# Flamingo block with sixteen experts: routing spread over the attention loop, expert stage fed by pairs of sequences

## What is computed

```
x = x + tanh(g_xattn) * attention(layernorm(x), ctx, ctx)
    # 16 heads of 16 channels, rope on q and k, keys within 64 tokens, softmax
x = x + tanh(g_ffn) * experts(layernorm(x))
    # per sequence: g = x @ w_router (256 x 16), probs = softmax(g), the top 2 of 16 experts per token
    # pos = how many earlier picks of this sequence went to the same expert
    #       (all first picks, in token order, come before all second picks)
    # a pick with pos < 16 puts the token into slot (expert, pos)
    # h = silu(slots @ w_gate[e]) * (slots @ w_fc[e]);  o = h @ w_proj[e]
    # token = sum of its two picks, each weighted by its probability
```

## Time and profile before

| | |
|---|---|
| Median of 3 runs | 1762.0 us (1760.66 to 1764.96) |
| Profiled execution, its own time | 1754.3 us |
| Span in the profile | 1752.5 us |
| TensorE busy | 1481.3 us (85%) |
| VectorE busy | 1408.6 us (80%) |
| ScalarE busy | 1146.4 us (65%) |
| GpSimd busy | 1086.1 us (62%) |
| Granted TensorE clock, mean | 0.960 |
| Memory traffic | 125.54 MB read, 83.89 MB written |

### The profile page before, as it was taken

One profiled execution on the slowest core, in us unless ns is written; L12 is line 12 of the kernel. 1 busy time (PEld: TensorE's weight loads), 2 busy tenths in 40 slices (PEclk: granted clock), 3 DMA queues, 4 the chain that ended last, 5 costly groups with the idle time before them and its releaser, 6 DMA issues. The chain is left out here.

```text
span 1752.5 us, 50746 instructions
## 1 busy us (share of the span) xinstructions
PE 1481.3 (85%) x16844; PEld 1195.2 (68%) x16844; DVE 1408.6 (80%) x2993; ACT 1146.4 (65%) x2321; POOL 1086.1 (62%) x1490
## 2 busy tenths in 40 slices
PE   3899999999999999999999999982199888888881
PEld 3676667777776676777676677761088888888881
DVE  3788888888888888878888888867878999999984
ACT  3777777777777777777777777764065555555550
POOL 3555656565655656565565656534638887888876
PEclk9999999999999999999999999995589999999995
DMA  3122121212222121212212121430037888888887
GB/s 94 50 76 75 61 89 60 90 60 84 65 67 82 60 90 60 90 60 78 71 62 88 60 90 60 137 119 30 15 106 245 260 261 258 261 273 263 264 261 223
DMA packets 156096, 210.21 MB, mean 120 GB/s; under 512 B 18688, under 2 KB 104832, under 8 KB 156032
## 3 DMA queue, kind: packets, MB, share of 16 engines
q1 hardware_dynamic: 125312, 142.36, 25.9%
q0 software_dynamic: 12288, 33.57, 6.7%
q10 hardware_dynamic: 18432, 33.56, 5.3%
HBM read 125.54 MB, written 83.89 MB: 119 GB/s over the span
## 5 line engine op out<-in xcount | busy, mean ns | idle before, releaser
L506 DVE TRANSPOSE_TENSOR_REDUCE part_max<-ST 128x16 f32<-128x512 f32 x512 | 321.3, 685 | 136.6 <-PE ST L685 136.6
L360 ACT ACTIVATE probs_t<-ST 128x512 f32<-128x512 f32 x512 | 264.4, 604 | 27.6 <-PE ST L700 27.4
L712 PE MATMUL PO<-probs_t,v_aug 128*32 128x128 f32 x4096 | 193.6, 284 | 67.9 <-ACT probs_t L360 55.4
L299 POOL TENSOR_TENSOR k_rot<-k_cos,k_sin 128x256 f32<-128x256 f32 x64 | 47.1, 736 | 268.5 <-DVE k_sin L544 268.5
L712 PEld LDWEIGHTS PO<-probs_t,v_aug 128*32 128x32 f32 x4096 | 88.9, 109 | 161.1 <-ACT probs_t L360 154.0
L1191 ACT ACTIVATE x_hi<-scaled 128x256 fp32r<-128x256 f32 x128 | 53.5, 418 | 214.8 <-DMA scaled<-xn_d 168.5
L401 ACT ACTIVATE at_hi<-F 128x512 fp32r<-128x512 f32 x64 | 38.2, 597 | 187.8 <-PE F L730 187.8
L1260 PE MATMUL GU<-we_hi,s_hi 128*128 128x256 f32 x512 | 155.4, 304 | 0.2 <-DVE s_lo L1250 0.2
L1154 POOL DMA_INDIRECT second<-eo_d,collect_row x128 | 123.0, 961 | 42.2 <-issue 28.6
L1163 POOL TENSOR_TENSOR x_lo<-scaled,x_hi 128x256 fp32r<-128x256 f32 x128 | 118.4, 925 | 49.3 <-ACT x_hi L1191 47.3
L1154 POOL DMA_INDIRECT first<-eo_d,collect_row x128 | 124.4, 972 | 37.3 <-issue 20.6
(11 more groups left out here) (158 smaller groups left out, 5610.7 us busy)
## 6 DMA issues: line engine op xcount, KB each, us to landing
eo_d<-eo ACTq DMA_DIRECT2D x128, 256.0 KB
x_in_sb<-x SPq DMA_DIRECT2D x64, 256.0 KB, 2.8
c_in_sb<-ctx_t SPq DMA_DIRECT2D x64, 256.0 KB, 2.9
xr_sb<-x SPq DMA_DIRECT2D x64, 256.0 KB, 4.0
x_d<-x SPq DMA_DIRECT2D x64, 256.0 KB, 4.0
xn_d<-xn SPq DMA_DIRECT2D x64, 256.0 KB, 4.2
scaled<-xn_d SPq DMA_DIRECT2D x128, 128.0 KB, 4.0
scaled<-x_d SPq DMA_DIRECT2D x128, 128.0 KB
```

Source lines behind the costliest of these rows:

```text
L360: act.activation(probs_t[:, b, i].rearrange("p j q -> p (j q)"), ST[i][:], ACT.Exp) \
L506: dve.tensor_reduce(part_max[:, i, 0], ST[i][:].rearrange("p (c l) -> p c l", l=32), AX_X, ALU.max, apply_transpose=True).then_inc(M["part ...
L712: last = pe.matmul(PO[32 * j:32 * j + 32, i * SEQ:(i + 1) * SEQ], v_aug[:, n.par, b, head], probs_t[:, b, i, j], start=True, stop=True)
```

## The change

Routing goes into attention's steps. Four sequences (two pairs, a `quad`) are routed together, in small instructions of 64 or 128 elements per partition. VectorE does some before `partial_max(s, 1)` (`route_early`) and some at the end of the step, before `partial_max(s + 1, 0)` (`route_late`); GpSimd, ScalarE and TensorE do the others, each one or more steps after what it needs:

```diff
+        def route_early(s):
+            if quad(s, 4):
+                find_first(quad(s, 4))
+                compare(quad(s, 4), 0)
+            if quad(s, 5):
+                expert_of(quad(s, 5), 0)
+            if quad(s, 6):
+                find_second(quad(s, 6))
+                compare(quad(s, 6), 1)
+            if quad(s, 7):
+                expert_of(quad(s, 7), 1)
+            if quad(s, 9):
+                rank_of(quad(s, 9))
+        def route_late(s):
+            if quad(s, 2):
+                find_peak(quad(s, 2))
+            if quad(s, 5):
+                drop_first(quad(s, 5))
+            if quad(s, 7):
+                mark_both(quad(s, 7))
+            if quad(s, 8):
+                ranks_of(quad(s, 8))
```

`quad(s, lag)` is the pair s - lag if that is odd and real, so even lags fall in odd steps. `find_first` is two reductions (sum and maximum), `drop_first` two instructions, the others one each. The one on TensorE comes last in its step, before the next scores:

```diff
+        def rank(s, n):
+            pe.wait_ge(M["marks_done"], n.half + 1)
+            wait_for(pe, M["ranked_done"], n.half)
...
+            pe.matmul(F2[:, 0:width], before[:], one, start=True, stop=True)
+            pe.matmul(F2[:, width:2 * width], ones_b[:], one, start=True, stop=False)
+            pe.matmul(F2[:, width:2 * width], before[:], two, start=False, stop=True).then_inc(M["ranks_done"], 1)
```

`width` is 64. TensorE's `untranspose(n, 1)` waits for `ranked_done` in addition, as both use bank F2. GpSimd's `route` (`less_peak`, twice `code_of`, `place_of`, lags 3, 5, 7, 9) stands between `residual` and `rotate`; ScalarE's `exp_logits` (lag 4) between `normed2` and `attention_head`. In the loop:

```diff
-        for c in range(-4, 2):
+        for c in range(-4, 12):
             step(Pair(0, c))
-        with eng.Fori(1, PAIRS // 2 - 2) as i:
+        with eng.Fori(6, PAIRS // 2 - 2) as i:
...
-        for c in range(PAIRS - 4, PAIRS + 2):
+        for c in range(PAIRS - 4, PAIRS + 9):
```

`routing_block` and `early_softmax` are gone. The expert weights are loaded in steps 4 to 8 (was 60 to 64) and split in steps 63 (`s.beyond == -1`) and 64 (`s.beyond == 0`), on ScalarE (`weight_heads`) and VectorE (`weight_rests`). To have room, attention's buffers that no step after 62 needs share their memory with `we_hi`, and `we_lo` lies over `w_in`. ScalarE's step:

```diff
+            if s.beyond == -1:
+                weight_heads(0, 3)
             if (s - 1).real:
                 attention_head(s - 1)
...
+            if s.beyond == 0:
+                weight_heads(8, 10)
             if (s - 2).real:
                 copy_normed2_t(s - 2)
...
+            if s.beyond == -1:
+                weight_heads(3, 8)
+            if s.beyond == 0:
+                weight_heads(10, CH)
```

VectorE's step:

```diff
                 shift_of(s, 0)
+            if s.beyond == -1:
+                weight_rests(0, 3)
...
+            if s.beyond == 0:
+                weight_rests(7, 8)
+            route_early(s)
...
                 residual_stats(s - 1)
+            if s.beyond == -1:
+                weight_rests(3, 7)
+            if s.beyond == 0:
+                weight_rests(8, CH)
```

```diff
-    LOAD, PICK, DISPATCH, GATE, HIDDEN, OUTPUT, FETCH, COLLECT = -13, -11, -9, 0, 2, 3, 12, 14
+    LOAD, PICK, HEAD, REST, DISPATCH, GATE, HIDDEN, OUTPUT, FETCH, COLLECT = -14, -11, -11, -10, -9, 0, 2, 3, 13, 15
...
+            if on(FETCH) and n.n % 2 == 0:
+                if n.n >= 6:
+                    for k in range(2):
+                        sp.wait_ge(y_out[(n.n + k) % 6], n.n // 6 * 16)
+                sp.dma_start(two(xr, n, 6), D["x1_d"][:, bass.ds(n.n, 2)]).then_inc(x1_in[n.n // 2 % 3], 16)
...
+                act.activation(gate[:, n.slot(2)], GU[n.slot(2)][:].rearrange("p (e f n) -> p e f n", e=2, f=2)[:, :, 0],
+                               ACT.Silu).then_inc(M["gate_done"], 1)
...
-                dve.scalar_tensor_tensor(out=th[:, n.slot(2)], in0=th[:, n.slot(2)], scalar=1.0, in1=gu[:, :, 0],
-                                         op0=ALU.add, op1=ALU.mult).then_inc(M["gated_done"], 1)
...
+                dve.tensor_tensor(flat(two(x_lo, n, 4)), flat(two(x_in_sb, n, 4)), flat(two(x_hi, n, 4)).bitcast(F32),
+                                  ALU.subtract).then_inc(M["x_lo_done"], 1)
```

More of the change, by code:

```diff
@@ L447, in normed2, with exp_logits, weight_heads @@
             last.then_inc(M["xn2_done"], 1)
+        def exp_logits(n):
+            act.wait_ge(M["less_done"], n.half + 1)
+            act.activation(four(scaled, n), four(scaled, n), ACT.Exp).then_inc(M["exp_done"], 1)
+        def weight_heads(first, end):
+            if first == 0:
+                act.wait_ge(M["w_landed"], 16 * (2 * KC + 1))
+                act.wait_ge(M["v_done"], PAIRS)
+                act.wait_ge(M["k_lo_done"], PAIRS)
+                act.wait_ge(M["ct_lo_done"], PAIRS)
+            for c in range(first, end):
+                act.activation(heads[:, c], raw[:, c], ACT.Copy).then_inc(M["heads_done"], 1)
         def step(s):
@@ L732, in transposes @@
             return last
+        weights = [(w_hi[:, w], w_lo[:, w]) for w in range(3)] + [(wo_hi[:], wo_lo[:])]
         def project(F, w, hi, lo, m):
@@ L1073, in expert_block @@
     second = sb("second", [P, 3, DIM])
-    ident, iota = T["ident2"], T["iota"]
-    place, collect_row, weight = T["place"], T["collect_row"], T["weight"]
+    ident, iota = T["ident"], sb("iota_sb", [P, SLOTS])
+    place, collect_row, weight = T["place"], T["code"][:].bitcast(I32), T["prob"]
+    kept, share = T["rank"], T["total"]
     half = EXPERTS * 2 * HID
@@ L1170, in step @@
         def step(unit, on):
-            n = unit(OUTPUT)
-            if on(OUTPUT):
-                act.wait_ge(M["eo_done"], n.n + 1)
-                wait_for(act, eo_out[n.turn(3)], (n - 3).landed(3))
-                act.activation(flat(eo[:, n.turn(3)]), EO[n.slot(2)][:], ACT.Copy).then_inc(M["eo_copied"], 1)
             n = unit(HIDDEN)
@@ L1183, in step @@
             if on(OUTPUT):
+                act.wait_ge(M["eo_done"], n.n + 1)
+                wait_for(act, eo_out[n.turn(3)], (n - 3).landed(3))
+                act.activation(flat(eo[:, n.turn(3)]), EO[n.slot(2)][:], ACT.Copy).then_inc(M["eo_copied"], 1)
+            n = unit(OUTPUT)
+            if on(OUTPUT):
                 act.wait_ge(M["eo_copied"], n.n + 1)
@@ L1186, in step @@
                     .then_inc(eo_out[n.turn(3)], 16)
-            n = unit(PICK)
-            if on(PICK):
-                act.wait_ge(x_in[n.turn(3)], n.landed(3))
-                wait_for(act, M["ds_done"], n.n - 1)
-                act.activation(x_hi[:, n.slot(2)], x_in_sb[:, n.turn(3)], ACT.Copy).then_inc(M["x_hi_done"], 1)
+            n = unit(HEAD)
+            if on(HEAD) and n.n % 2 == 0:
+                act.wait_ge(x_in[n.n // 2 % 2], pair_landed(n, 2))
+                wait_for(act, M["ds_done"], n.n - 2)
+                act.activation(flat(two(x_hi, n, 4)), flat(two(x_in_sb, n, 4)), ACT.Copy).then_inc(M["x_hi_done"], 1)
             n = unit(GATE)
```

520 lines of the change are left out of this document (259 added, 261 removed).

## The result

The changed kernel takes 1751.3 us (median of 4 runs, 1749.8 to 1752.8), the kernel before beside it 1763.0 (1760.7 to 1765.0). The ratio is 0.9936, with a 95% interval of 0.9917 to 0.9954: 0.6% less time, clear of the noise but small, where 1696 was forecast. The profiled execution has a span of 1750.4 us against 1752.5 before. The two spans differ by 2.1 us and the medians by 11.6, since the profiled execution of the kernel before (1754.3 us) was faster than any other run of it here (1756.2 to 1767.3).

What follows compares the result with a forecast made beforehand. Each stage has another limit; full expert units have four resources near 3.5 us. Terms +20 +3 -46.9 +1 +1 -47 +2.5 = -66.4 from 1754.3 give 1688, or 1696 on the median's footing; range 1664 to 1734.

Steps and rivals of the forecast that it cites:

- the routing stage: Between last logits and first pick: 56.4 us replaced by 9.5 (28 small instructions, handoffs, a block end), -46.9 us.
- splitting: Splitting the expert weights moves from the routing stage into steps 63 and 64: +3 us, bounds 0 and 7.
- start, expert start and tail: Setup +1 us, expert start +1, tail +2.5 from collecting one unit later and gathers pacing the end.
- So TensorE is next, with DMA just under it ... I take 3.05: Full expert units: TensorE sets the pace at 2.90 us; with some waits 3.05 instead of 3.53, -47 us.
- The 0.17 us that larger pieces should take off the queues: Expert-unit loads: 2 KB instead of 1 KB pieces cut DMA time per unit from 3.00 to 2.83 us.
- Rival 1: Expert units: DMA keeps the pace, a unit stays at about 3.4 us, total 1730; chance 0.15.
- Rival 4: Expert units: VectorE and GpSimd block each other, 4.2 us a unit, +66 instead of -47, total 1809; chance 0.04.
- Even late: 0.99 less 0.34 less the 0.3 absorbed, 0.35 late: Attention loop, end of even steps: three VectorE instructions overrun their slot by 0.35 us per two steps.
- TensorE's 0.3: Attention loop: three uncovered bf16 routing matmuls with their waits cost TensorE 0.3 us per two steps.
- My 0.33 us per instruction: Attention loop: assumed time of each of 13 small VectorE routing instructions per two steps, between 0.25 and 0.44.
- the five of the odd step: Attention loop, odd early slot: five VectorE instructions take 1.65 us against 1.60, 0.05 late.

Runs made afterwards that it cites:

- e4: Changed kernel with each load of xn2 and x1 issued as two transfers of one sequence instead of one of two: 1748.2 us.
- e8: Changed kernel with gathers issued for the first three sequences only (output not the reference's): 1655.1 us.
- e11: Changed kernel with the second gather left out after the first three sequences (output not the reference's): 1664.3 us.
- e14: Changed kernel with the second gather bringing half a row per token after the first three sequences (output not the reference's): 1673.8 us.
- e16: Changed kernel's attention and routing with the expert units of the kernel before, OUTPUT one unit later (4) and the factor 0.5 restored: 1749.8 us.
- e3: Changed kernel with x1 loaded only for the first six sequences (output not the reference's): 1746.5 us.
- e13: Changed kernel with OUTPUT one unit later (4; FETCH 14, COLLECT 16): 1685.4 us.
- e12: Changed kernel with x_lo on GpSimd again in place of VectorE: 1770.1 us.
- e9: Changed kernel with GpSimd's residual (xb) in even steps waiting for VectorE's marks of the step before: 1737.2 us.
- e15: Changed kernel with GpSimd's residual waiting for marks, rest made after marks, and OUTPUT one unit later: 1663.0 us against 1757.7 for the kernel before, ratio 0.9455.
- e7: Changed kernel with TensorE's three small routing matmuls issued twice: 1752.3 us.
- e6: Changed kernel with drop_first, mark_both and all of route_early placed right after shift_of(s, 0), where GpSimd waits for k_sin: 1866.7 us.
- e2: Changed kernel's attention and routing with the expert units of the kernel before, output weights lacking the factor 0.5: 1750.1 us.
- e5: Kernel before with only the changed kernel's expert stage, turns and buffer layout: 1767.6 us beside 1765.4.
- e1: Changed kernel with drop_first and mark_both moved from the end of even steps to before the second maxima of even steps: 1752.3 us.

## Why the prediction was wrong

The parts at the ends came out: the routing stage -45.3 (forecast -46.9; the small instructions took 7.6 us where I had 9, and 3.5 us of waiting for `iota`, which I did not have, made up for it by luck), splitting +5.2 (3, bounds 0 to 7), start, expert start and tail within 3.1 us each. The stage has one ACT_TABLE_LOAD for Silu, 1.28 us at 1266.52, and none per unit, as the Trainium skill (ScalarE: Activation LUTs, Table sets) had led to expect.

**Expert units: the step that failed is "So TensorE is next, with DMA just under it ... I take 3.05".** Most parts of that step held. The collects take 0.48 us (0.477 to 0.479), VectorE and GpSimd have the slack I gave them, `x_hi` no longer waits for its load, and given one more unit of lag the pace is 2.90, at my lower bound, with DMA at 0.95 (I had said 2.83 of 2.90 us would be busy). The 0.17 us that larger pieces should take off the queues did not come (0.05, and e4 has the same with small ones), but decided nothing. What the sum left out is not a resource but a distance: HT of a unit and its EO lie one turn apart. In the timeline from 1504 on HT's row ends at 1504.83 and EO starts at 1506.55, 1.72 us; `h_hi` starts at 1504.87 and `h_lo` ends at 1506.21:

```profile
1504.45 0.38 PE L1348 MATMUL HT<-ident_sb,gate 128*128 128x128 f32 x2
...
1505.79 0.42 DVE L1277 TENSOR_TENSOR h_lo<-HT,h_hi 128x256 fp32r<-128x256 f32 x1
...
1506.55 0.28 PE L1327 MATMUL EO<-we_hi,h_hi 128*128 128x256 f32 x1
```

Any lateness of over 0.34 us is TensorE's. The distance alone does not hold the pace, since e8, e11 and e14 reach 2.87 with it; it takes the distance and the late signals, at which the prediction had nothing. A list of busy times can't show that; TensorE's waits by line could have, since in the kernel before too they stood ahead of EO, and I had put the whole of the 3.53 down to loads and busy engines. The run with the later OUTPUT and the old units (e16) shows that the old form had a limit of its own at 3.50, with ScalarE waiting for loads. The change took that limit away and met the next one, by coincidence, at the same pace.

Rival 1 gave a unit of 3.4 and a total of 1730, the right sign of the error for a wrong reason: e3 and e13 rule out the traffic as the limit. Rival 4 did not come about: the collects were not stretched with x_lo on VectorE, and e12 shows that they are when it is GpSimd's. (It had gathers running 75% of the time; two of 0.95 us in 3.53 are 54%.)

**Attention: "Even late: 0.99 less 0.34 less the 0.3 absorbed, 0.35 late", and TensorE's 0.3.** Four sizes were off. The three instructions take 1.30 us, not 0.99, since `marks` runs beside `xb`. Nothing is absorbed: 1.30 - 0.34 is 0.96, and the five of the odd step take 609.78 to 611.46, 1.68 against a slot of 1.60, 0.08; together 1.04 of the 1.09 measured. By the same sum e9 gives 0.82 - 0.34 + 0.08 = 0.56 (measured 0.61) and e15 0.59 - 0.34 + 0.08 = 0.33 (0.37). TensorE's matmuls cost nothing (e7). And 24 pairs of steps paid, those of the loop, not 30: 24 x 1.08 is 26, nearly all of the 26.9 measured, where 30 would be 32, so this error hid part of the others. My 0.33 us per instruction is the mean of the odd slot (1.68 / 5), by luck, with two of the five stretched. The Trainium skill (SBUF — State Buffer, Who interferes with whom) has a VectorE instruction with two inputs in SBUF contend with a GpSimd instruction that reads SBUF. I had weighed this rule for the expert units, where the trace spoke against it for gathers, and e11, e13, e14 and e15 still do (collects of 0.48 us beside gathers); it belonged in the attention loop, and there the trace agrees: 0.77 against 0.29 us for `marks` (e9, with `xb` held back), 0.53 against 0.23 for `same_as` (0.23 behind the last pair and in e6, with GpSimd idle).

**What stays open**: what makes a signal late. Late signals are there with two full gathers per unit and OUTPUT at 3 (also without x1, with small loads, with gathers spaced), fewer with x_lo on GpSimd, and absent from 1350 to 1600 with one gather, with one and a half, or with the new units and OUTPUT at 4; in e16, the old units with OUTPUT at 4, about a quarter of the recorded ones are 0.5 to 1.2 us late, and what they cost can't be seen behind the wait for loads. In the changed kernel TensorE's stall and the late signals come together; which of them starts the other was not separated. All runs with late signals also have the new buffer layout, e2 and e5 included, and no run changed that alone; by itself it does not bring them, since e13 has it too. What is shown is that a unit of slack removes both from the new units.

## What to carry to other kernels

When all engines are under 85% busy and the pace has not moved, stop adding up busy times and count the turns between producer and consumer: the cheapest fix here was a 4 in place of a 3. Remove two limits that lie close together in one change, or neither shows a gain. Before small VectorE instructions go into an idle slot, look at what GpSimd runs there; holding GpSimd's instruction back by 0.6 us (e9) was worth more than moving VectorE's (e1).

## What was not expected of the hardware

- TensorE's increments of semaphores came up to 3.8 us behind the modelled end of their matmuls, and five of them within 0.31 us of each other. From 1350 to 1600, with one and a half gathers or fewer per unit, or with one unit more of slack for the new units, none came late.
- The step is sharp: 2.88 us a unit with 1.5 gathers, 3.53 with 2, and 2.90 with 2 and more lag.
- DMA engines ran at 0.95 and 315 GB/s through a window of 250 us with TensorE at 98.8%.
- A VectorE instruction of 64 elements per partition was stretched up to threefold (0.21 to 0.64 us) by a GpSimd tensor instruction beside it.
